# Centring the output weights so that attention's norm needs no mean, and summing every steady tile's exponentials as they are made

## The reference, cut to what matters

```
combined = concatenate([comp_out * g0, sel_out * g1, win_out * g2], axis=-1)
out = combined @ Wo + bo
out = out * 0.5 + hidden_states * 0.5
mu = out.mean(-1); var = out.var(-1)
s = (out - mu) * rsqrt(var + 1e-6)
y = x + s * silu(ffn(xn))
```

## Time and profile before

| what | value |
|---|---|
| median of 3 runs | 310.98 us (310.61 to 312.87) |
| profiled execution: its time | 310.19 us |
| profiled execution: its span | 308.4 us |
| busy: DVE, ACT, PE, POOL | 271.2, 241.8, 241.9, 231.6 us |
| mean granted clock of TensorE | 0.952 |

### The profile page before, as it was taken

The page is one execution under the profiler, slowest core; times in us unless marked ns, Lnnn a source line. Parts: engine busy times, 40 slices in busy tenths (PEclk is TensorE's granted clock), DMA queues, the critical chain, the costliest instruction groups (busy, mean ns, idle before and its releaser), DMA issues.

```text
span 308.4 us, 7810 instructions
## 1 busy us (share of the span) xinstructions
PE 241.9 (78%) x1493; PEld 172.4 (56%) x1493; DVE 271.2 (88%) x2579; ACT 241.8 (78%) x1031; POOL 231.6 (75%) x355
## 2 busy tenths in 40 slices
PE   0389788569888888899888988898888897885851
PEld 0344333358466656677565756575656674664741
DVE  6449999993999999999999999999999999995134
ACT  1425557635999899989988998999899989997532
POOL 8855610633867889998899889978998898887671
PEclk9999999956999999899999999999999999999795
DMA  8910000000000000010000001000100010001002
GB/s 176 257 46 0 2 3 0 0 1 2 1 1 3 1 3 1 2 35 3 1 27 11 3 0 36 2 3 1 37 1 0 4 35 0 5 1 34 2 0 68
DMA packets 11111, 6.26 MB, mean 20 GB/s; under 512 B 1332, under 2 KB 10552, under 8 KB 11064
## 3 DMA queue, kind: packets, MB, share of 16 engines
q1 hardware_dynamic: 9736, 5.12, 6.3%
q10 hardware_dynamic: 1328, 0.66, 1.1%
HBM read 3.68 MB, written 2.10 MB: 19 GB/s over the span
## 4 chain that ended last, share of the span: by engine, by line
DVE 63%; POOL 12%; PE 12%; issue 9%; ACT 3%; POOLq 0%; ACTq 0%; DVEq 0%
DVE rest L1074 22%; DVE top L1083 13%; DVE top L1063 13%; DVE last L1107 6%; POOL squareT L456 2%; POOL wgt L469 2%; DVE slot_gap L1092 1%; PE f_bank L1388 1%; PE sim L1395 1%; PE c_bank L1388 1%; PE sim L1358 1%; DVE st L998 1%; DVE den L1049 1%; PE s_bank L1381 1%; POOL rstd L418 1%
## 5 line engine op out<-in xcount | busy, mean ns | idle before, releaser
L1074 DVE MATCH_REPLACE8 rest<-top,sim 128x32 f32<-128x32 f32 x512 | 85.7, 180 | 0.2 <-issue 0.2
L1083 DVE MAX8 top<-rest 128x8 f32<-128x32 f32 x512 | 53.7, 177 | 0.7
L1063 DVE MAX8 top<-sim 128x8 f32<-128x32 f32 x496 | 50.9, 178 | 2.2 <-PE sim L1395 2.2
L755 ACT ACTIVATE prob<-drop 128x50 f32<-128x50 f32 x184 | 42.1, 247 | 0.0
L456 POOL TENSOR_TENSOR squareT<-sideT 100x512 bf16<-100x512 bf16 x31 | 33.1, 1069 | 11.1 <-ACT sideT L690 11.1
L1074 DVE MATCH_VALUE_LOAD rest<-top,sim 128x8 f32 x512 | 40.9, 80 | 0.3
L441 POOL TENSOR_TENSOR past<-gap,last 128x400 f32<-128x400 f32 x31 | 26.8, 864 | 18.3 <-DVE last L1107 18.3
L755 ACT ACTIVATION_READ_ACCUMULATOR prob<-drop 128x1 f32 x184 | 37.6, 204 | 0.0
L463 POOL TENSOR_TENSOR drop<-gap,out_by 128x400 f32<-128x400 f32 x31 | 32.0, 1034 | 7.1 <-ACT out_by L681 7.1
L1395 PE MATMUL sim<-sim_w,xT_all 128*128 128x512 f32 x64 | 34.0, 613 | 0.8 <-issue 0.8
L469 POOL TENSOR_TENSOR wgt<-prob,rden 128x400 f32<-128x400 f32 x31 | 26.9, 869 | 9.6 <-DVE rden L1053 9.6
(11 more groups left out here) (262 smaller groups left out, 746.0 us busy)
## 6 DMA issues: line engine op xcount, KB each, us to landing
out<-y_sb SPq DMA_DIRECT2D x7, 256.0 KB, 2.3
x_sb<-in_L_attn_hidden_states SPq DMA_DIRECT2D x2, 256.0 KB, 3.8
fwq_sb<-in_L_ffn_Wq ACTq DMA_DIRECT2D x2, 256.0 KB, 5.9
x_sb<-in_L_attn_hidden_states SPq DMA_DIRECT2D x1, 512.0 KB, 5.5
wc_sb<-in_L_attn_Wc SPq DMA_DIRECT2D x1, 256.0 KB
out<-last_y SPq DMA_DIRECT2D x2, 128.0 KB, 1.8
wo_sb<-in_L_attn_Wo SPq DMA_DIRECT2D x1, 192.0 KB
keys_sb<-in_L_ffn_keys ACTq DMA_DIRECT2D x1, 128.0 KB, 3.4
```

What stands on the lines that cost most here:

```text
L755: last = nc.scalar.activation(prob[d][:, h, :], drop[:, h, :], ACT.Exp, scale=-1.0, accum_out=den[d][:, h:h + 1])
L1063: last = nc.vector.max(top[d][:, v, 0:8], sim_bank[d][:, bass.ts(v, KEYS)])
L1074: last = nc.vector.match_replace(out=rest[:, v, :], in_to_replace=top[d][:, v, 0:8], in_values=sim_bank[d][:, bass.ts(v, KEYS)], imm_value ...
L1083: last = nc.vector.max(top[n % 2][:, v, 8:16], rest[:, v, :])
```

## The change

`Wo` and `bo` are centred over their 128 output columns once, by ACT, in the start-up's step `b == 3` (`centre_outputs`, 10 activations), after a wait for all late loads. The centred `bo` is sent to its four places by four DMAs that SP issues after a wait. The residual is no longer `ident` times `xn_all` but `xT_all` times `off_mean`, a matrix of one on the diagonal less 1/128 everywhere, which POOL makes among its constants. So attention's output has mean zero: `row_sums`, `nmean2` and `nmr2` go, the squares take no bias, and `s_norm` is a copy with a scale only. `summed` is now true for the last three tiles alone, so the six other tiles' exponentials are made in 8 instructions with accumulated sums, and DVE doesn't reduce them.

```
@@ -127,7 +127,11 @@
         wc_sb = sb("wc_sb", [P, RATIO, D])
-        wo_sb = sb("wo_sb", [P, 3, D])
+        wo_in, wo_spare, wo_sb = (sb(n, [P, 3, D]) for n in ("wo_in", "wo_spare", "wo_sb"))
+        bo_in, bo_spare, bo_sb = (sb(n, [1, D]) for n in ("bo_in", "bo_spare", "bo_sb"))
+        wo_sum, wo_mean = (sb(n, [P, 3]) for n in ("wo_sum", "wo_mean"))
+        bo_sum, bo_mean = (sb(n, [1, 1]) for n in ("bo_sum", "bo_mean"))
+        off_mean = sb("off_mean", [P, D])
         bq_sb, bqs_sb, bk_sb, bv_sb, bc_sb = (sb(n, [P, 1]) for n in ("bq_sb", "bqs_sb", "bk_sb", "bv_sb", "bc_sb"))
@@ -202,9 +206,8 @@
         pT_cs = sb("pT_cs", [P, 2, P])
-        spare = sb("spare", [P, 2, TB, D])
-        sum2, nmean2, sq2, var2, rstd2, nmr2 = (
-            sb(n, [P, TB]) for n in ("sum2", "nmean2", "sq2", "var2", "rstd2", "nmr2"))
+        spare = sb("spare", [P, TB, D])
+        sq2, var2, rstd2, nmr2 = (sb(n, [P, TB]) for n in ("sq2", "var2", "rstd2", "nmr2"))
         s_norm = [sb(f"s_norm{i}", [P, TB, D]) for i in range(2)]
@@ -243,7 +246,7 @@
             sem(n) for n in ("keys_in", "fwq_in", "zw_in", "down_in", "w_late"))
-        FWQ_DMAS, ZW_DMAS, DOWN_DMAS, LATE_DMAS = 2, 2 + 4, 2, 9 + TB + 1
+        FWQ_DMAS, ZW_DMAS, DOWN_DMAS, LATE_DMAS = 2, 2 + 4, 2, 9 + 1 + 1
         bqs_done = sem("bqs_done")
@@ -279,8 +282,9 @@
             sem(n) for n in ("s_ready", "max_done", "p_exp", "rinv_done", "rgate_done", "p_scaled"))
-        out_ready, sums2, mean2, squares2, norm2_step, norm2_ready, s_done = (
-            sem(n) for n in ("out_ready", "sums2", "mean2", "squares2", "norm2_step", "norm2_ready", "s_done"))
+        out_ready, squares2, norm2_step, norm2_ready, s_done = (
+            sem(n) for n in ("out_ready", "squares2", "norm2_step", "norm2_ready", "s_done"))
+        wo_step, bo_put = sem("wo_step"), sem("bo_put")
         y_step, y_free, y_done, y_stored = sem("y_step"), sem("y_free"), sem("y_done"), sem("y_stored")
@@ -307,7 +311,7 @@
 
-            return n >= TILES - 3 or (n > TB and n % TB == 2)
+            return n >= TILES - 3
 
@@ -339,12 +343,15 @@
             sp.dma_start(wc_sb[:, :, :], wc.rearrange("(r p) n -> p r n", p=P)).then_inc(w_late, 16)
-            sp.dma_start(wo_sb[:, :, :], wo.rearrange("(r p) n -> p r n", p=P)).then_inc(w_late, 16)
-            for j in range(TB):
-                sp.dma_start(vww[WKEYS:WKEYS + 1, j, :], bo.rearrange("(a n) -> a n", a=1)).then_inc(w_late, 16)
+            sp.dma_start(wo_in[:, :, :], wo.rearrange("(r p) n -> p r n", p=P)).then_inc(w_late, 16)
+            sp.dma_start(bo_in[:, :], bo.rearrange("(a n) -> a n", a=1)).then_inc(w_late, 16)
             sp.wait_ge(consts, CONSTS)
...
                          ).then_inc(w_late, 16)
+
+            sp.wait_ge(wo_step, 3)
+            for j in range(TB):
+                sp.dma_start(vww[WKEYS:WKEYS + 1, j, :], bo_sb[:, :]).then_inc(bo_put, 16)
 
@@ -378,6 +385,7 @@
             nc.gpsimd.tensor_copy(ident16[:, :], ident[:, :])
+            nc.gpsimd.tensor_scalar(off_mean[:, :], ident[:, :], -1.0 / D, None, ALU.add)
             nc.gpsimd.memset(neg_half[:, :], -0.5)
@@ -536,10 +544,8 @@
                 nc.gpsimd.tensor_scalar(var2[:, :], sq2[:, :], 1.0 / D, 4e-6, ALU.mult, ALU.add).then_inc(norm2_step, 1)
-                pool.wait_ge(norm2_step, 2 * b + 1)
-                nc.gpsimd.tensor_tensor(rstd2[:, :], var2[:, :], neg_half[:, 0:TB], ALU.pow).then_inc(norm2_step, 1)
-                pool.wait_ge(norm2_step, 2 * b + 2)
-                nc.gpsimd.tensor_tensor(nmr2[:, :], nmean2[:, :], rstd2[:, :], ALU.mult).then_inc(norm2_ready, 1)
+                pool.wait_ge(norm2_step, b + 1)
+                nc.gpsimd.tensor_tensor(rstd2[:, :], var2[:, :], neg_half[:, 0:TB], ALU.pow).then_inc(norm2_ready, 1)
 
@@ -702,6 +708,23 @@
 
+            def centre_outputs():
+
+                for r in range(3):
+                    last = nc.scalar.activation(wo_spare[:, r, :], wo_in[:, r, :], ACT.Identity,
+                                                accum_out=wo_sum[:, r:r + 1])
+                nc.scalar.activation(bo_spare[:, :], bo_in[:, :], ACT.Identity,
+                                     accum_out=bo_sum[:, :]).then_inc(wo_step, 1)
+                act.wait_ge(wo_step, 1)
+                nc.scalar.activation(wo_mean[:, :], wo_sum[:, :], ACT.Copy, scale=-1.0 / D)
+                nc.scalar.activation(bo_mean[:, :], bo_sum[:, :], ACT.Copy, scale=-1.0 / D).then_inc(wo_step, 1)
+                act.wait_ge(wo_step, 2)
+                nc.scalar.activation(bo_sb[:, :], bo_in[:, :], ACT.Identity, bias=bo_mean[:, 0:1]
+                                     ).then_inc(wo_step, 1)
+                for r in range(3):
+                    last = nc.scalar.activation(wo_sb[:, r, :], wo_in[:, r, :], ACT.Identity, bias=wo_mean[:, r:r + 1])
+                last.then_inc(wo_step, 1)
+
             for b in range(B):
@@ -711,6 +734,9 @@
                     last.then_inc(zw_done, 1)
+                if b == 3:
+                    act.wait_ge(w_late, 16 * LATE_DMAS)
+                    centre_outputs()
                 if b == 4:
@@ -767,21 +793,12 @@
 
-            def row_sums(b):
+            def row_squares(b):
 
...
                 for j in range(TB):
-                    last = nc.scalar.activation(spare[:, 0, j, :], out_bank[:, bass.ts(j, D)], ACT.Identity,
-                                                accum_out=sum2[:, j:j + 1])
-                last.then_inc(sums2, 1)
-
-            def row_squares(b):
-                act.wait_ge(sums2, b + 1)
-                nc.scalar.activation(nmean2[:, :], sum2[:, :], ACT.Copy, scale=-1.0 / D).then_inc(mean2, 1)
-                act.wait_ge(mean2, b + 1)
-                for j in range(TB):
-                    last = nc.scalar.activation(spare[:, 1, j, :], out_bank[:, bass.ts(j, D)], ACT.Square,
-                                                bias=nmean2[:, j:j + 1], accum_out=sq2[:, j:j + 1])
+                    last = nc.scalar.activation(spare[:, j, :], out_bank[:, bass.ts(j, D)], ACT.Square,
+                                                accum_out=sq2[:, j:j + 1])
                 last.then_inc(squares2, 1)
@@ -789,8 +806,8 @@
                 for j in range(TB):
-                    last = nc.scalar.activation(s_norm[b % 2][:, j, :], out_bank[:, bass.ts(j, D)], ACT.Identity,
-                                                bias=nmr2[:, j:j + 1], scale=rstd2[:, j:j + 1])
+                    last = nc.scalar.activation(s_norm[b % 2][:, j, :], out_bank[:, bass.ts(j, D)], ACT.Copy,
+                                                scale=rstd2[:, j:j + 1])
                 last.then_inc(s_done, 1)
@@ -929,7 +946,6 @@
                     take_topT(n - 1)
-                    row_sums(b - 1)
                     take_sides(n - 2)
@@ -1527,6 +1543,7 @@
 
+                pe.wait_ge(wo_step, 4)
                 o = fill(m_unit(b, U_VWW), U_VWW % 2)
@@ -1556,10 +1573,11 @@
                         pe.wait_ge(f_out, min(b, B - 2))
+                    else:
+                        pe.wait_ge(bo_put, 16 * TB)
                 for j in tiles:
                     o = out_bank[:, bass.ts(j, D)]
-                    mm(o, ident[:, :], xn_all[:, bass.ds(b * TB + j, 1), :].rearrange("p a d -> p (a d)"),
-                       start=True, stop=False)
+                    mm(o, xT_all[:, bass.ts(b * TB + j, P)], off_mean[:, :], start=True, stop=False)
                     if j == 0:
```

## The result

The changed kernel takes 317.14 us (median of 4 runs, 314.86 to 319.0), beside 310.94 of the kernel before in the same comparison: ratio 1.018, 95% interval 1.010 to 1.026 (ranges behind the ratios below are such intervals). The forecast was 310.7, its range ended at 313.1. The profiled execution took 317.4 us with a span of 315.6, which is 7.2 more than before. (Of all executions compared in this document two, one of the kernel before with 1178.52 us and one of the kernel of experiment 8 with 581.91, took far longer than their like; the ratios leave them out.)

A forecast was written before the change was run, and what follows sets the result against it. The prediction took DVE to bound the kernel (63% of the chain), a DVE-ACT-DVE chain nearly as long. 310.19 + 0.5 (off_mean) - 0.8 (reductions) = 309.9 us profiled; the median is 0.79 higher, 310.7; range 308.2 to 313.1.

The forecast's parts named there:

- PE behind the longer ACT turn: j == 2 turns: attention_out waits for silu_parts, 1.39 us later; PE still reaches pair_gaps in time, 0.2 us to spare, no cost.
- a falling clock: Start-up, where PE lies on the chain: TensorE's clock falling elsewhere, named among what could mislead most; no size.
- Rival 3: j == 2 turns: PE's 0.2 us to spare is missing, DVE's wait grows, 0.4 more in each of six: 313.1 us; chance 0.06.
- Reductions gone from DVE: Six of nine reductions go, 0.48 us each; a new 0.35 us wait for gap leaves 0.13 each, 0.8 us gained.
- Rival 1: j == 2 turns: second chain is shorter, six reductions come through in full: 308.6 us; chance 0.2 including what lies towards the forecast.
- What goes from ACT: ACT per batch row: 2.01 us removed against 1.39 added; row_sums' 1.02 is not on the way that counts.
- `off_mean`: Start-up, POOL's constants ahead of the first norm: one more constant, +0.5 us, bounds 0.44 and 0.72.
- lock of the shared port: Start-up: POOL's off_mean and DVE's two-input additions taking the port in turn, ending it up to 0.4 us later.
- `centre_outputs`: ACT's start-up, before the norm of row 5: 2.4 to 2.9 us of work under 3.04 us of idle cover, no cost.
- rival 2: Start-up: centre_outputs with its waits exceeds 3.04 us and reaches the chain through the norm of row 7: 313.2 us; chance 0.1.

The follow-up runs named there:

- experiment 8: The kernel of experiment 6 with off_mean made later by POOL, plus ten PE products nobody reads in the start-up: 306.8 us, ratio 0.9805.
- experiment 2: The changed kernel plus two PE products of 240 columns, never read, in front of attention_out's wait: 310.19 us, ratio 0.9937.
- experiment 6: The changed kernel with silu_parts after two of eight exponentials, and take_topT ahead of side_of in ACT's j == 2 turns: 308.58 us, ratio 0.988.
- experiment 5: The kernel of experiment 4 with silu_parts after two of the eight exponentials: 312.73 us, ratio 1.002.
- Experiment 3: The changed kernel with the centring alone, the six tiles' sums staying on DVE: 311.61 us, ratio 1.0007.
- experiment 4: The kernel before with the sums part of the change alone, without the centring: 317.9 us, ratio 1.019.
- experiments 6 to 9: experiment 6; that with off_mean made later by POOL (308.17 us); experiment 8; that with ACT's order side_of, take_topT, out_by_of (307.02 us).

## Why the prediction was wrong

**The step that failed** stands under "PE behind the longer ACT turn": "This costs nothing, with 0.2 us to spare." The lateness was right: `attention_out` waited for `silu_parts` as forecast, and at full clock PE does catch up, which turns 10 and 18 and experiment 2 show (wait for `gap` 0.24, stretch 8.79). What the step left out is what the granted clock does after PE has stood idle: I took PE's durations of the earlier trace rows as fixed, while in four turns most of them grew from 0.39 to 0.63 or 0.64 us, and then 3.2 us of work ahead of `pair_gaps` had no 0.2 us to spare. Price: 6.5 us, of the 7.2 by which the profiled span grew. The prediction named a falling clock as what could make it wrong, but in the start-up, and gave it no case of its own in the range; the idle itself could be had from the earlier trace rows: 173.28 + 1.39 - 173.54 = 1.13 us. And the trace of the kernel before had a fall of the clock in the steady turns: in one batch row of six, after a wait of PE of 0.90 us.

```profile
128.05 0.20 PE L1439 MATMUL f_bank<-count_s,sideT 101*128 101x100 bf16 x1 [0.90 <-POOL squareT L456]
```

```profile
120.76:150.29 29.53, 26.58 (x172) 20.01 (x172) 29.35 (x306) 28.01 (x127) 26.46 (x37) 0.94 0.04 11
130.00:132.00 2.00, 2.00 (x10) 1.85 (x10) 2.00 (x22) 1.73 (x5) 2.00 (x3) 0.50 0.15 43
150.29:179.83 29.54, 25.40 (x172) 18.77 (x172) 29.36 (x307) 27.86 (x127) 26.41 (x37) 1.00 0.04 11
```

That fall (the middle line; the columns are those of the earlier trace rows) cost nothing: the batch row with it takes 29.53 us, the next one, without it, 29.54. What makes a fall dear is where it comes; in the `j == 2` turns of the changed kernel DVE's next read hung on the slowed products.

**Rival 3** came nearest: DVE's wait for `gap` grew above 0.5 us, by way of PE. But it was priced at 0.4 us a turn for lack of slack, where the clock makes it 1.33 to 2.52.
The Trainium skill (TensorE: Matmul & The Clock Gate, section "HAM oscillation — how this bites in real kernels") describes this for kernels whose PE waits between bursts of matmuls, for DMAs above all: it is clocked down, and the next burst starts at the low clock. The traces agree on what follows the 1.1 us (0.54 and 0.50 in the windows from 147.00), and they add that it is no rule for each single wait. The waits of that section's main example are longer than the 1.1 us here, so by it no fall was to be expected; the measurement decides.

**Reductions gone from DVE:** right, the old L1049 (L1065 now) appears three times for nine. Of the forecast net gain of 0.13 us a batch row 0.16 came where the clock held (8.79 for 8.95), with a marked wait of 0.24 for the forecast 0.35. The two fit better than they look: without a wait L1092 starts 0.08 us before its predecessor's recorded end (150.29 in turn 14 before, where that end is 150.37), so a marked 0.24 is a delay of 0.32. Rival 1, the full 0.48, did not occur; experiment 6 shows that it needs more than `topT` in time.

**What goes from ACT:** the 1.02 us of `row_sums` was left out of the way that counts, since `topT` goes over PE. Right for the changed kernel, but experiment 5 adds the other half: with `row_sums` kept, ACT's way becomes the longer by 0.39 us (wait 0.62 against 0.23). Taking 1.02 away gains the first 0.39, up to the point where the way over PE takes over.

**`off_mean`:** forecast +0.5, measured +0.48 at the `slot_gap` read of turn 1. The timelines of POOL and DVE, which answer to the earlier trace rows:

```profile
2.71 0.55 POOL L388 TENSOR_SCALAR off_mean<-ident 128x128 f32<-128x128 f32 x1
...
12.16 1.12 DVE L1046 TENSOR_SCALAR xn_all<-x_sb,rstd,nmr 128x128 f32<-128x128 f32 x4 [4.55 <-POOL nmr L430]
```

It took 0.55 us, the 0.56 taken for 128 columns. The Trainium skill's lock of the shared port (SBUF — State Buffer, section "SBUF: two separate sides") would have added up to 0.4; it began beside DVE's additions, and no such stretch is seen. DVE's sixteen additions took 1.64 us for the 1.52 of the earlier trace rows, which held nothing back; what lengthened them stays open.

**`centre_outputs`:** right, rival 2 did not occur. ACT's timeline, answering to the earlier trace rows:

```profile
27.41 0.30 ACT L714 ACTIVATE wo_spare<-wo_in 128x128 f32<-128x128 f32 x1
...
29.34 0.97 ACT L725 ACTIVATE wo_sb<-wo_in,wo_mean 128x128 f32<-128x128 f32 x3
30.21 1.63 ACT L660 ACTIVATE xn_all<-x_sb,nmr,rstd 128x128 f32<-128x128 f32 x4
...
34.14 1.65 ACT L660 ACTIVATE xn_all<-x_sb,nmr,rstd 128x128 f32<-128x128 f32 x4 [0.56 <-POOL nmr L430]
```

It takes 30.21 - 27.41 = 2.80 us, and the norm of row 7 still waits 0.56 for POOL. That norm starts 0.48 later than in the earlier trace rows, which is POOL's delay by `off_mean`. The norm of row 5 is later than forecast, by 3.26 us for 2.1 to 2.5, and the copy of row 4 by 2.23 for 1.0 to 1.4, since ACT reaches `centre_outputs` 0.9 late already; the cover was enough for that too. Experiment 3 agrees: the centring alone measures no difference.

**Not foreseen:** the clock in the rest of the start-up (+0.75 us), and the last stretch (+0.34), which belongs to the sums (8.06 us in experiment 3, 9.03 in experiment 4). The first is no steady cost: in the second trace of the changed kernel the stretch of 14.31 us took 13.36.

## What to carry to other kernels

When an edit makes a matrix engine wait where it did not, price the wait twice: once by its slack at full clock, and once with all of PE's work behind it at the low level, since an idle of one microsecond was enough here to cost up to 2.9 where DVE's next read hung on PE, while the fall in the kernel before cost nothing. The repair is cheap: put the short work that PE waits for ahead of the long work on the releasing engine, or let PE do products nobody reads in the gap. And after such a repair look at what is late next, since a queue moved forward on one engine puts the items it passed behind it.

## What the hardware showed that I had not expected

- The same idle has two outcomes. PE stood idle 1.09 to 1.11 us at the same place of the same list in 18 turns of three traces; the clock fell in 13 of them: four and three of six in two executions of the changed kernel, six of six in experiment 4. Its length alone doesn't decide: PE waited as long at other places, 1.16 to 1.27 us ahead of `transpose_sides` in experiments 6 to 9 and 1.14 to 1.19 us just behind the `slot_gap` read of the six turns in the kernel before, and the clock stayed at 1.00 there each time. What does decide the traces don't tell, and no experiment here varied the length of the idle step by step. The scatter of the changed kernel (314.5 to 319.4 us) fits with a varying number of falls: its three slowest executions (319.0 to 319.4) have the lowest mean granted clocks, 0.908 to 0.919, the other six 0.928 to 0.944. But only two of the nine have a trace.
- Added work makes a kernel faster: two products a batch row took 6.6 us off the changed kernel's `j == 2` stretches, ten in the start-up took one stretch from 13.20 us down to 11.06 in one trace and 11.97 in another.
- The fall is not over when the idle is: PE was busy all the time from 147 to 153 us and the granted clock stayed at 0.50 to 0.54.
